# Self attention of a decoder kernel: softmax inverses copied over rows by DMA instead of spread by TensorE

## The reference

```python
cp = leaky_relu(einsum('btd,cd->btc', representations, Wc) + bc)
q = cp[..., :128].reshape(B, T, 16, 8)
k = cp[..., 128:256].reshape(B, T, 16, 8)
v = cp[..., 256:].reshape(B, T, 16, 64)
scores = einsum('bqhd,bkhd->bhqk', q, k) / SCALE
attn = softmax(scores, axis=-1)
out = einsum('bhqk,bkhd->bqhd', attn, v).reshape(B, T, 1024)
proj = leaky_relu(einsum('btv,dv->btd', out, Wo) + bo)
return representations + proj
```

## Time and profile before

| what | value |
|---|---|
| median of 3 runs | 2145.32 us (2144.95 to 2147.92) |
| profiled execution | 2149.18 us, span 2147.3 us |
| mean granted TensorE clock | 0.916 of full speed |
| TensorE matmuls busy | 1829.5 us, 85% of the span |
| VectorE busy | 1031.1 us, 48% |
| ScalarE busy | 889.6 us, 41% |
| GpSimd busy | 515.7 us, 24% |
| chain that ended last, TensorE's share | 65% |

### The profile page before, as it was taken

The page is one execution under the profiler, slowest core; times in us unless marked ns, Lnnn a source line. Parts: engine busy times, 40 slices in busy tenths (PEclk is TensorE's granted clock), DMA queues, the critical chain, the costliest instruction groups (busy, mean ns, idle before and its releaser), DMA issues.

```text
span 2147.3 us, 27241 instructions
## 1 busy us (share of the span) xinstructions
PE 1829.5 (85%) x10505; PEld 1046.0 (49%) x10505; DVE 1031.1 (48%) x2074; ACT 889.6 (41%) x1422; POOL 515.7 (24%) x577
## 2 busy tenths in 40 slices
PE   4698898977998988979898888898988978989788
PEld 3344654633344545543455564434544643455456
DVE  5576466543653353346443534463435255643442
ACT  2222222213644454336353633463635425635443
POOL 2475276300440021006300300071003002700120
PEclk8799999977999999989999998899998988999999
DMA  7000000000000000000000000000000000000000
GB/s 198 1 1 0 0 0 0 0 0 0 1 1 1 1 1 1 6 0 1 1 1 1 1 1 6 1 1 1 1 1 1 1 6 1 1 1 1 1 1 5
DMA packets 18259, 13.27 MB, mean 6 GB/s; under 512 B 7643, under 2 KB 14783, under 8 KB 18143
## 3 DMA queue, kind: packets, MB, share of 16 engines
q1 hardware_dynamic: 17951, 11.65, 2.0%
q10 hardware_dynamic: 192, 0.02, 0.0%
HBM read 10.55 MB, written 1.05 MB: 5 GB/s over the span
## 4 chain that ended last, share of the span: by engine, by line
PE 65%; issue 10%; DVE 8%; ACT 6%; POOL 5%; POOLq 5%; DVEq 1%; DMA 0%; SPq 0%; ACTq 0%
PE PSUM L1256 6%; PE PSUM L1422 5%; PE PSUM L1414 5%; PE PSUM L1300 5%; PE PSUM L422 4%; PE PSUM L1324 3%; PE PSUM L378 3%; POOLq L864 2%; PE PSUM L1387 2%; PE PSUM L1310 2%; POOLq L862 2%; POOL OTA L866 2%; POOL OTA L861 2%; PE PSUM L352 2%; PE PSUM L400 2%
## 5 line engine op out<-in xcount | busy, mean ns | idle before, releaser
L577 DVE TENSOR_REDUCE negmax<-PSUM 128x2 f32<-128x1024 f32 (+3 forms) x256 | 256.4, 1016 | 122.5 <-PE PSUM L384 66.2
L234 POOL TENSOR_TENSOR rstd<-var,neg_half 128x4 f32<-128x4 f32 (+1 forms) x33 | 33.5, 1015 | 1006.0 <-DVE var L224 920.6
L559 ACT ACTIVATE PTA<-PSUM 128x1024 f32<-128x1024 f32 (+1 forms) x224 | 214.1, 963 | 100.4 <-PE PSUM L422 99.6
L2008 DVE TENSOR_REDUCE nmax<-PSUM 128x1 f32<-128x589 f32 x128 | 98.7, 771 | 177.0 <-PE PSUM L1301 177.0
L1256 PE MATMUL PSUM<-PTA,VA 128*64 128x512 f32 x512 | 146.3, 649 | 4.7 <-ACT OTA L538 2.2
L1669 ACT ACTIVATE PTA<-PSUM,V 128x512 f32<-128x512 f32 x128 | 87.9, 687 | 134.2 <-PE PSUM L1414 131.2
L1300 PE MATMUL PSUM<-KMA,QXA 128*128 128x512 f32 x256 | 136.4, 615 | 5.7 <-ACT VA L1628 3.1
L639 POOL TENSOR_TENSOR QXA<-QXA,PTA 128x1024 f32<-128x1024 f32 x56 | 132.7, 2370 | 35.5 <-ACT PTA L559 32.0
L422 PE MATMUL PSUM<-QSTACK,KSTACK 64*128 64x512 f32 (+3 forms) x512 | 111.3, 454 | 22.5 <-ACT PTA L559 9.0
L1414 PE MATMUL PSUM<-YT,W 128*128 128x512 f32 x256 | 125.1, 637 | 0.0
L1422 PEld LDWEIGHTS PSUM<-W,PTA 128*128 128x128 f32 x1024 | 118.2, 192 | 10.0 <-issue 9.9
(11 more groups left out here) (411 smaller groups left out, 3593.6 us busy)
## 6 DMA issues: line engine op xcount, KB each, us to landing
W<-in_L_ffn_W_dram SPq DMA_DIRECT2D x1, 2048.0 KB
out_dram<-X SPq DMA_DIRECT2D x4, 256.0 KB, 2.3
PTA<-in_L_attn_Wc_dram SPq DMA_DIRECT2D x1, 640.0 KB
PTA<-in_L_attn_Wo_dram SPq DMA_DIRECT2D x1, 512.0 KB
Wkv<-in_L_xattn_Wkv_dram SPq DMA_DIRECT2D x1, 512.0 KB
KMA<-in_L_attn_ttt_proj_dram SPq DMA_DIRECT2D x1, 256.0 KB
QXA<-in_L_ffn_w_up_dram SPq DMA_DIRECT2D x1, 256.0 KB
QXA<-in_L_ffn_w_down_dram SPq DMA_DIRECT2D x1, 256.0 KB
```

The source lines that it names most:

```text
L559: A.activation(probs, PSUM[:, at:at + 2, 0:probs.shape[2]], ACT.Exp).then_inc(m_exp, 1)
L577: last = Vv.tensor_reduce(negmax[:, s % 2, t, :], PSUM[:, k:k + 2, at:at + a.width(t)], AX.X, ALU.max, negate=True)
L2008: Vv.tensor_reduce(nmax[:, 0, i % 3:i % 3 + 1], PSF[:, at:at + XK], AX.X, ALU.max, negate=True).then_inc(s_max, 1)
```

## The change

Stacks 0 to 5 of each batch lose their spread on TensorE. In its place SP waits for the inversion of the stack and issues 8 DMAs, each of which reads one row of 128 inverses (512 B) on one partition of PB and writes it to the 64 partitions of its head, into one of two buffers of [128, 512]: the tile YT, idle during the loop, and columns 256 to 767 of PB. `inv_pair` moves to columns 0 to 255 of PB. SP also waits until the buffer's last reader, the normalisation of stack s - 2, is done. `normalise` of these stacks waits for all 8 copies, reads both inputs from SBUF, and runs one pass later: in pass s VectorE normalises stack s - 3, and stack 5 after the loop, behind the inversion of stack 6. Stacks 6 and 7 keep the spread. The sums of a stack now wait only for the inversion before, not for a normalisation, since bank 7 has no other reader.

```diff
@@ sums
                     if s:
-                        pe.wait_ge(m_norm, b * PAIRS + s)
+                        pe.wait_ge(m_inv, b * PAIRS + s)
@@ spread
                 pe.wait_ge(m_inv, b * PAIRS + s + 1)
-                pe.wait_ge(m_rows, a.stacks(b, min(s + 4, PAIRS)))
@@ the loop on TensorE
                 value(s, 1)
-                if s >= 2:
-                    spread(s - 2)
                 scores_T(s, 3)
@@ VectorE
             def normalise(s):
                 dve.wait_ge(m_outs, a.groups(b, s + 1))
-                dve.wait_ge(m_spread, b * PAIRS + s + 1)
-                Vv.tensor_tensor(OT[:, s, :], OT[:, s, :], bank(1 if s == PAIRS - 1 else 7), ALU.mult).then_inc(m_norm, 1)
+                if s < PAIRS - 2:
+                    dve.wait_ge((m_replica0, m_replica1)[s % 2], 8 * 16 * (b * (PAIRS - 2) // 2 + s // 2 + 1))
+                    factors = inv_rows[s % 2]
+                else:
+                    dve.wait_ge(m_spread, 2 * b + s - PAIRS + 3)
+                    factors = bank(1 if s == PAIRS - 1 else 7)
+                Vv.tensor_tensor(OT[:, s, :], OT[:, s, :], factors, ALU.mult).then_inc(m_norm, 1)
@@
                 tile(ahead + 2)
-                if s >= 2:
-                    normalise(s - 2)
+                if s >= 3:
+                    normalise(s - 3)
                 tile(ahead + 3)
                 if s:
                     invert(s - 1)
+            normalise(PAIRS - 3)
             invert(PAIRS - 1)
@@ buffers
-        inv_pair = [PB[:, i, 0:P] for i in range(2)]
+        PBF = PB[:, :, :].rearrange("p r n -> p (r n)")
+        inv_pair = [PBF[:, P * i:P * (i + 1)] for i in range(2)]
+        inv_rows = [YT[:, :], PBF[:, 2 * P:2 * P + SEQ]]
@@ SP
             for b in range(BATCH):
+                for s in range(PAIRS - 2):
+                    sp.wait_ge(m_inv, b * PAIRS + s + 1)
+                    if s >= 2:
+                        sp.wait_ge(m_norm, b * PAIRS + s - 1)
+                    for e in range(2):
+                        for t in range(QT):
+                            at = t * LANE + 16 * e
+                            row = inv_pair[s % 2][at:at + 1, :]
+                            load(inv_rows[s % 2][e * VD:(e + 1) * VD, t * P:(t + 1) * P],
+                                 bass.AP(row.tensor, row.offset, [[2 * XK, 1], [0, VD], [1, P]]), (m_replica0, m_replica1)[s % 2])
                 sp.wait_ge(s_rowdone, b + 1)
```

More of the change, by code:

```diff
@@ L271, in decoder_kernel @@
         s_xi, s_xsp, s_xn = (sem("x1_" + n) for n in ("sums_inverted", "spread", "values_normalised"))
-        (m_parts, m_picked, m_stacked, m_scores, m_max, m_split, m_turned, m_rows, m_scoresT, m_exp, m_acc01,
+        (m_parts, m_picked, m_stacked, m_scores, m_max, m_split, m_turned, m_rows, m_scoresT, m_exp, m_acc01, m_replica0, m_replica1,
          m_acc, m_sums, m_inv, m_spread, m_norm, m_values, m_outs) = (sem("m_" + w) for w in (
             "parts", "picked", "stacked", "scores", "max", "max_split", "max_turned", "max_rows", "scores_T",
-            "exp", "sum01", "sum0123", "sums", "inverted", "spread", "normalised", "values", "values_copied"))
+            "exp", "sum01", "even_replicated", "odd_replicated", "sum0123", "sums", "inverted", "spread", "normalised", "values", "values_copied"))
         m_tri = sem("m_triangle_cleared")
```

## The result

The changed kernel takes **2168.31 us** (median of 12 runs, 2157.83 to 2170.3), the kernel before 2147.22 beside it (12 runs, 2143.93 to 2158.88): ratio 1.0084, 95% interval [1.007, 1.0099]; the ratio is worked out from all runs, not from the two medians. It is slower by 0.84%, where 0.25% faster was forecast, and lies outside the range. The profiled execution took 2166.64 us, its span is 2164.9, the mean granted clock 0.905 against 0.916.

A forecast was written before the change was run, and what follows sets the result against it. Two almost equal branches bound each stack: value and spread on PE, maxima rows and exponential on ACT. Gains of 0.56 + 0.06 + 0.69 = 1.31 us per batch, 5.2 over four, gave 2140.1 us on the median's scale; range 2137 to 2156.

The forecast's parts named there:

- the two branches: In a stack's 8.93 us cycle, value and spread on PE nearly equal maxima rows and exponential on ACT; 0.14 us freed.
- the release of 0.06: At the fourth chunk of transposed scores, PE starts 0.06 us after ACT's exponential ends.
- the closed gap of pass 7: In pass 7, without maxima rows before the exponential, the fourth chunk of transposed scores may start 0.69 us earlier.
- the sum of 1.31 us per batch: Self attention's gain per batch: 0.56 in passes 2 to 5, 0.06 in pass 6, 0.69 in pass 7.
- The chain's 23 us: Rival, 4%: all 24 removed spreads come off the path at 0.97 us each, 23.3 us, giving 2122.
- c: Time per copy once SP's copies stream; taken near the 0.43 us issue, free up to 1.14.
- The copies come late: Rival, 22%: copies delay normalise 5 at the stage's end, from c = 1.14; 2151 us at 1.2, 2170 at 1.3.
- The estimate of 1.2 us: For c: a 32 KB copy reading one partition at 27.2 GB/s, just past the free limit, making the sum a loss.
- VectorE never waits for the copies: Expected sign: SP's 48 issues per batch land in under 5 us and VectorE never waits for them.
- The collision: Rival, 3%: in the stacks normalise waits for a GpSimd addition, 2.2 us late, net +12 or 2157 us.
- I let the shift run through to the projection (L1268) and the layer after it: Behind the released points no ACT, DVE or GpSimd wait holds PE, so 1.31 us per batch, 5.2 over four, carries through.
- The clock falls: Rival, 3%: thinner stacks lower PE's clock, about 1.7 us per fall; once per batch 2147 us, in every stack 2181.

The follow-up runs named there:

- e2: The kernel before with all spreads kept and the 192 copies added beside them, not used for the result: 2145.37 us, ratio 0.9978.
- e6: The kernel before plus 10 idle matmuls per batch in the gaps of the causal opening: 2141.99 us, ratio 0.9972.
- e12: The kernel before plus idle matmuls in the openings of both causal stage and self attention (10 and 24 per batch): 2134.46 us, ratio 0.9933.
- e1: The changed kernel without its 192 copies, normalise of stacks 0 to 5 multiplying by a constant weight tile: 2160.72 us, ratio 1.0048.
- e5: The changed kernel plus 10 idle matmuls per batch in the gaps of the causal opening: 2138.49 us, ratio 0.9955.
- e9: The changed kernel measured once more, unchanged, with a second profile: 2161.53 us, ratio 1.0068.
- e10: The changed kernel with 10 idle matmuls per batch in the causal opening, without the 192 copies (constant tile instead): 2139.55 us, ratio 0.9961.
- e11: The changed kernel plus idle matmuls in the openings of both causal stage and self attention (10 and 24 per batch): 2132.32 us, ratio 0.9924.
- e4: The kernel before plus 6 idle matmuls per batch (1.3 us) before the last projection of the self attention: 2175.05 us, ratio 1.0116.
- e3: The changed kernel plus 6 idle matmuls per batch (1.3 us) before the last projection of the self attention: 2144.43 us, ratio 0.9979.
- e7: The changed kernel plus 12 idle matmuls per batch (2.6 us) before the last projection of the self attention: 2175.8 us, ratio 1.0124.
- e8: The changed kernel plus 3 idle matmuls per batch (0.6 us) before the last projection of the self attention: 2144.49 us, ratio 0.9982.

## Why the prediction was wrong

**What held.** The reading of the two branches: a removed spread frees 0.14 us in the steady cycle and not 0.97, since ACT's exponential ends just before; the release of 0.06; the closed gap of pass 7. Of the sum of 1.31 us per batch the traces show 1.34 (mean of the four batches) from the first inversion to the last addition, and the same in every pair of this study: that part takes 64.4 us in before, e2, e6 and e12, and 63.1 in after, e1, e5, e9, e10 and e11, in each batch. So the whole self attentions, 1.5 shorter in the first batch and 1.1 in the third and fourth, differ from it only by what their openings, ahead of the first inversion, do; the 5.4 longer of the second batch lies there too. The chain's 23 us were not there.

**The copies.** c was taken near the issue of 0.43; the issue alone is 0.62 here, and the eight of a stack are done 5 us into a cycle of 8.78. "The copies come late" needed c = 1.14 and did not happen. The estimate of 1.2 us from the Trainium skill ("SBUF — State Buffer", Door 1: The DMA port swizzle) would have given a queue that grows from stack to stack; the next stack's issues begin one cycle later each time, and a copy lands in 3.2 us, so this trace doesn't bear it out. "VectorE never waits for the copies" was wrong by 1.31 us behind the loop, under cover.

**The collision** was sized about rightly (a product 2.2 us late, measured 2.52 - 0.68 = 1.84 late) and placed wrongly. In the stacks normalise (588.50) is there before GpSimd's addition (589.10), and both keep their lengths; the 0.2 us for which GpSimd was to wait don't show. Once per batch normalise comes while an addition runs, which began at 615.44 and lasted 4.88 us, to 620.32. It took 2.52 us and ended at 620.87, 0.55 behind the addition, so it did its work of 0.68 at the end. The Trainium skill ("SBUF — State Buffer", Who interferes with whom) calls the shared ports an exclusive lock, and this row agrees. It is hidden.

**The step that failed** is "I let the shift run through to the projection (L1268) and the layer after it". I looked behind each released point for a wait that another engine would set, and found none. But what lies behind runs at TensorE's granted clock, and that is not a constant of the code. The rival "The clock falls" had the right kind of cause and was looked for where the work was removed. In the stacks the clock stayed at 1.00, with PE busy for 8.00 of 8.78 us. It fell some 150 us later, in an opening that the change doesn't touch, for 10 us more per batch: at half speed that is worth up to 5 us, and the stages measure 3.4 longer. Four of those are the 13.8 us. The earlier trace rows showed the stretch: that second pair of windows, 6.51 busy of 9 us at 1.00 and then 0.81, was this very opening. I priced one such fall, at 1.7 us in the stacks, and did not ask what it would do if the opening itself came at another time.

**What the saved time is worth.** The cross attention's opening takes back a part wherever the self attention got shorter: 0.7 us per batch in after, and 0.6 to 0.9 between e12 (116.3 to 116.6 us) and e11 (116.9 to 117.2). The first 15 us behind the self attention, before and after:

```profile
640.70:655.70 15.00, 8.45 (x19) 3.99 (x19) 5.41 (x17) 3.17 (x5) 1.02 (x1) 0.77 0.00 1
```

```profile
636.90:651.90 15.00, 8.48 (x17) 4.08 (x18) 4.81 (x17) 3.17 (x5) 1.02 (x1) 0.66 0.00 1
```

Equal busy time, 0.77 and 0.66. One group of eight matmuls carries the difference; it starts 7.8 us behind the addition in both and takes 0.64 us longer in after:

```profile
648.51 5.43 PE L1278 MATMUL PSUM<-YT,Wq 128*128 128x512 f32 x8 [0.87 <-ACT YT L1586]
```

```profile
644.67 6.07 PE L1293 MATMUL PSUM<-YT,Wq 128*128 128x512 f32 x8 [0.87 <-ACT YT L1601]
```

e4, with 1.3 us *added*, has a cross attention longer still, 117.6 us, and e3, the changed kernel moved back by its six matmuls, has the 116.5 to 116.6 of before, so this again goes with the place in time. So the change is worth 2 to 4 us where the causal opening is filled, not 5.2.

**What orders the causal stages.** One reading of the traces does. Each causal stage starts while the clock is still at its low level, from a fall before it, and how long it stays there tells where the stage lies against the clock's own steps. These windows run from 3.5 to 5.5 us behind the stage's first matmul: the second batch of before, then the first and the second of e9:

```profile
1177.20:1179.20 2.00, 2.00 (x13) 1.66 (x11) 1.41 (x3) 0.60 (x1) 0.00 (x0) 0.88 0.00 0
```

```profile
758.50:760.50 2.00, 2.00 (x12) 1.83 (x11) 1.41 (x3) 0.60 (x1) 0.00 (x0) 0.75 0.03 8
1174.59:1176.59 2.00, 2.00 (x11) 1.88 (x10) 1.41 (x3) 0.60 (x1) 0.00 (x0) 0.66 0.00 0
```

A mean of 0.88 puts the end of the low stretch at 3.5 + 2 x 2 x 0.12 = 4.0 us; 0.75 gives 4.5 and 0.66 gives 4.9. The stages took 69.2, 67.5 and 72.7 us. In the nine kernels without filling of the opening (before, after, e1 to e4, e7 to e9) the 36 causal stages fall in order: ends of 3.9 to 4.06 us go with 68.8 to 69.2 in nine and with 67.3 in two, ends of 4.18 to 4.50 with 67.3 to 67.5 in five, and ends of 4.54 and later with 72.2 to 72.9 in all twenty. In e5, e10 and e11, with the gaps filled, eight stages have ends of 4.54 to 4.90 and still take 67.4 to 67.9. So the filling did not merely move the stage to a lucky place.

**What stays open.** Why these ends go with these times, and by what sum a shift of the self attention could have been turned into such an end ahead of the run. Nor is it shown whether the copies make the fall in the second self attention come more often, if that is what the slower runs have in common: eleven of the 18 runs of the changed kernel took 2166 us or more (nine of 12 in the first measurement, two of 6 in e9), none of the ten of e1. Nor is it shown why after's second self attention lost 6.6 us in one execution; its opening stood at the low level for 30 us instead of 16 to 20, without a difference in the work.

## What to carry to other kernels

Before trusting a gain of a few us in a program with stages, look for stretches behind the change where PE waits often and the granted clock has fallen even once; there the same code has several prices, here 67.4, 68.9 and 72.4 us, and 0.6 us of idle work per batch (e8) was enough to pick another. Test a small change with such stretches filled with idle matmuls in both kernels: that takes most of the lottery out of the comparison (not all: the fourth self attention of e10 took 119.3 us beside 114.7 to 116.3 in the others, the third of e12 118.1 beside 115.0 to 116.0), and here the filling itself was worth more (23 to 30 us on the changed kernel) than the change (2 to 4 us). Subtract the wait that lies under a removed step before pricing it: 16 matmuls that held TensorE for 0.97 us freed 0.14.

## What the runs showed of the hardware

Adding 1.3 us of TensorE work per batch made a kernel of 2168 us (2162 in e9) 24 (17) us faster, and made one of 2147 us (2154 beside that run) 28 (21) us slower; both go with the granted clock (0.905 to 0.918, 0.916 to 0.907).

The kernel before is subject to it too. Beside e9 its 17 runs went from 2143.26 to 2156.11, with mean clocks of 0.919 down to 0.914: most near 2145, four above 2153. Beside e1 it was the other way round, 18 of 27 above 2152.

The Trainium skill ("TensorE: Matmul & The Clock Gate", Part 1: The HAM clock gate) says that the clock gate follows TensorE's recent busy time on a clock of its own that a kernel's start does not reset. The pair of windows in e9 agrees: the same pauses, once without and once with a fall.

Copies of one SBUF row to 64 partitions issue at 0.62 us each on SP (plain copies inside SBUF at 0.60) and land in 3.2, close to the 2.8 of a plain copy of 16 KB, though each reads one partition 64 times.
